# Output transposes moved from TensorE and ScalarE to VectorE, one mask product for two blocks, biases moved to ScalarE, in a two-layer attention and mixture-of-experts kernel

## The chip, the cores and the metric

The kernel runs on one core of a Trainium2 chip. A core has a matrix engine (TensorE, in the profile PE; its weight loads are PEld), three engines for elementwise work (VectorE or DVE, ScalarE or ACT, GpSimd or POOL), a queue engine (SyncE or SP) and 16 DMA engines. Each engine runs its own instruction list in order and waits on semaphores. The metric is the device time of one launch in microseconds (us), lower is better. Three runs of the kernel before took 2808.42, 2810.91 and 2811.84 us, median 2810.91 us.

## The reference: what is computed

The input `x` is 16 sequences of 512 tokens with 128 channels, float32. Two layers follow, and every head has 8 channels:

```python
xn = layernorm(x)                                   # 16 x 512 x 128
# layer 0, attention A: 16 query heads over 4 key/value heads, with biases, softmax over all 512 keys
a  = softmax((xn@wq.T+bq) . (xn@wk.T+bk) / sqrt(8)) . (xn@wv.T+bv) @ wo.T + bo
# layer 0, block M: rmsnorm, keys and values through a latent of 64 channels with a layernorm,
# rotary positions, 16 heads, causal softmax; then 4 experts, each token goes to its best one
latent = layernorm(rms(xn)@Wdkv.T)*ln_g + ln_b
m  = xn + causal_softmax(rope(q) . rope(latent@Wuk.T)) . (latent@Wuv.T) @ Wo.T
m  = m + expert[argmax(rms(m)@gate.T)](rms(m))      # 128 -> 512 -> 128, relu
x  = x + a + m
xn = layernorm(x)
# layer 1, attention B: 16 query heads over one key/value head, with biases; and a gated layer of 384
x  = x + attention_B(xn) + (silu(xn@wg.T) * (xn@wu.T)) @ wd.T
```

## The kernel before: tiling, stages and what sets the order

One sequence of 512 tokens (4 tiles of 128) is a batch; there are 16. A batch passes through three attentions, named M (causal, with the latent), A (grouped) and B (layer 1). The heads of an attention are taken in 4 groups `g` of 4 heads. For each group:

1. `score_max` computes scores of 128 queries against the keys, 16 units `u` a group. TensorE writes them to a PSUM bank with four matmuls side by side, each on 32 columns of the array (`in_columns`). VectorE takes the row maximum (line 972; for M with the causal mask added, line 977).
2. `shift_split` (GpSimd), `shift_turn` (TensorE, ScalarE, SyncE) turn the maxima and put them as rows 72 and 73 of the queries.
3. `score_exp` computes the scores again, transposed and shifted by the maximum, in 16 units a group (10 for M, where two causal blocks share one bank). For M a product of `late_keys` with the identity adds the mask on the diagonal block. ScalarE writes the exponentials to `probs` (line 1217).
4. `probs_v` multiplies them with the values, with a column of ones for the sum, into the one PSUM bank `pv`. It holds two groups, for 32 rows a head: 16 for the even group's values and 16 for the odd group's.
5. After every second group: `out_copy` copies `pv` to `osb` (ScalarE, line 1223), `out_turn` turns it with four 128x128 transposes (TensorE, line 748), and VectorE divides by the sums (lines 985 and 992) into `otok`, tokens on partitions. After both pairs of groups `o_turn` turns `otok` back (TensorE line 623, ScalarE line 1229) into `oT`, and `o_proj` multiplies with the output weights.

So a batch has six `out_copy` and `out_turn`, and three `o_turn`.

The order of the work is a table of times. `stages()` puts each step at a time in units of which a period has 12 (`PERIOD`); one unit is one group of score maxima. `START` places M at 3, A at 7 and B at 23, and `LEAD` adds 1 to every time, so the maxima of M stand at 4 to 8, of A at 8 to 12 and of B at 24 to 28, which is 0 to 4 of the period two periods later. `score_exp` follows `lag` = 1.986 units behind. Every engine runs the steps that it has a part in, in the table's order; `LATE` moves a step's place on one engine alone. One period handles parts of three batches. The walk repeats it 18 times, and the first and the last periods are only partly filled.

PSUM has 8 banks. One is `pv`; the other 7 are handed out round robin in the table's order, with the same banks in every period. `last_user` makes the taker of a bank wait for the step that read it last. A query or key in `full_q` or `full_k` passes through GpSimd's `split` into three bfloat16 parts and by DMA (`pack`) into the operand rows. The table places `m_lat_turn` at 1.55, `o_turn` of A at 2.521, `out_copy` of A at 0.174 and 2.174 (with `LEAD`, modulo 12).

Of the kernel before, what the change touches and what calls it, by code (L numbers as in the profile page):

```python
# [102 lines left out]
for _n, _w in (("a_bv", 32), ("a_bo", 128), ("gate_b", EXPERTS), ("b_bv", HD), ("b_bo", 128)):  # L103
# [36 lines left out]
def stages():  # L140
# [92 lines left out]
def spare_users(name, *args):  # L233
# [8 lines left out]
        "out_turn": [(f"{a}_otok", g + 1)] if name == "out_turn" else [],  # L242
        "o_turn": [(f"{a}_oT", 1)], "o_proj": [({"M": "x2_ready", "A": "gqa_added", "B": "y_ready"}.get(a), 1)],
# [12 lines left out]
def kernel_program(nc, x, w_all, w_lat, v_all, r_all, consts, wx, xq, yq, wi_up, wi_down, rope, out):  # L256
# [7 lines left out]
    with ctx:  # L264
# [64 lines left out]
        otok = sb("otok", [P, TILES, D])  # L329
# [270 lines left out]
        def _(pe):  # L600
# [222 lines left out]
            def ff_down(b):  # L823
                m = misc_bank(b, "res_b", 1)
                pe.wait_ge(sig["ff_hid"], total(b, "ff_hid"))
                for t in range(TILES):
                    for c in range(FCH):
# [12 lines left out]
        def _(v):  # L840
            turn_mx, turn_full, turn_otok, turn_factored = {}, {}, {}, {}
            turn_hid = {}
# [76 lines left out]
            def m_lat_turn(b):  # L919
# [594 lines left out]
```

## Time and profile before

| | |
|---|---|
| median of 3 runs (lowest, highest) | 2810.91 us (2808.42, 2811.84) |
| profiled execution, its own time | 2806.16 us |
| its span, first to last instruction | 2804.4 us |
| PE busy | 2618.0 us, 93% |
| DVE busy | 2303.3 us, 82% |
| ACT busy | 1735.6 us, 62% |
| POOL busy | 813.7 us, 29% |
| mean granted TensorE clock | 0.977 of full |
| DMA | 191.23 MB, mean 68 GB/s |

Busy time is the time in which at least one instruction of the engine is in flight. An instruction's duration contains a tail that overlaps the next one, so that work which is issued back to back takes less than the sum of the durations. The distance from the start of one to the start of the next is then its price. An engine that waits less than such a tail still counts as busy.

### The profile page before, as it was taken

The numbers are of one execution on the slowest core, as the hardware profiler recorded it, in microseconds if no ns is written. First come the engines' busy times: TensorE is split into PE (matmuls) and PEld (weight loads), VectorE is DVE, ScalarE is ACT, GpSimd is POOL, SyncE is SP. The second block draws the span as 40 slices with busy tenths as digits, with TensorE's granted clock in tenths as the row PEclk, the third lists the DMA queues.
The fourth block names the chain that finished last, engine by engine and source line by source line (L and its number), as shares of the span: only waits on it lengthen the run. The fifth ranks groups of instructions, "written<-read, shape, count | busy, mean of one in ns | idle before, by whom it ended". The sixth has DMA issues, their size and how long they took to land. (4 is left out here: it accounts for less than half of the span.)

```text
span 2804.4 us, 120631 instructions
## 1 busy us (share of the span) xinstructions
PE 2618.0 (93%) x50864; PEld 1434.5 (51%) x50864; DVE 2303.3 (82%) x6003; ACT 1735.6 (62%) x3538; POOL 813.7 (29%) x1385
## 2 busy tenths in 40 slices
PE   5969999999999999999999999999999999999958
PEld 2445464645546465464645546464554646456432
DVE  5758889798898979889797987979889897988735
ACT  1725757666576666757666575766757666675825
POOL 4132422223241222423133242222324122242120
PEclk7979999999999999999999999999999999999987
DMA  3041221403112041221304122140312204132120
GB/s 99 7 129 32 79 75 32 125 25 109 54 59 91 26 137 29 90 74 43 106 25 131 36 82 72 32 125 25 110 53 66 83 27 136 28 96 67 39 67 6
DMA packets 168044, 191.23 MB, mean 68 GB/s; under 512 B 24614, under 2 KB 150736, under 8 KB 167504
## 3 DMA queue, kind: packets, MB, share of 16 engines
q1 hardware_dynamic: 163408, 175.12, 20.7%
q0 software_dynamic: 4096, 8.40, 1.1%
q8 instruction: 402, 6.59, 1.0%
q14 instruction: 138, 1.13, 0.1%
HBM read 84.18 MB, written 16.25 MB: 36 GB/s over the span
## 5 line engine op out<-in xcount | busy, mean ns | idle before, releaser
L1217 ACT ACTIVATE probs<-bank 128x512 f32<-128x512 f32 x2688 | 1461.7, 598 | 667.5 <-PE bank L617 661.0
L972 DVE TENSOR_REDUCE mx<-bank 128x1 f32<-128x512 f32 x2048 | 1281.4, 681 | 65.2 <-PE bank L617 52.2
L977 DVE CUSTOM_DVE_ANT_0 bank<-bank,mask 128x128 f32<-128x128 f32 (+3 forms) x1024 | 478.5, 517 | 106.6 <-PE bank L617 100.4
L617 PE MATMUL bank<-kp_B,qp_B 72*32 72x512 bf16 x4096 | 442.9, 392 | 18.8 <-issue 9.4
L617 PE MATMUL bank<-qp_B,kp_B 74*32 74x512 bf16 x4096 | 415.4, 384 | 2.2 <-ACT probs L1217 1.6
L617 PE MATMUL bank<-qp_A,kp_A 74*32 74x512 bf16 x4096 | 408.2, 380 | 6.7 <-DVE mx L972 6.1
L617 PE MATMUL bank<-kp_A,qp_A 72*32 72x512 bf16 x4096 | 384.2, 381 | 14.8 <-DVE mx L972 7.5
L1362 POOL TENSOR_SCALAR nms<-mx 128x16 bf16<-128x16 f32 x192 | 39.8, 207 | 1043.2 <-DVE mx L977 510.2
L617 PE MATMUL bank<-kp_M,qp_M 72*32 72x128 bf16 (+3 forms) x4096 | 314.7, 311 | 28.2 <-DMA kp_M<-parts_k 20.4
L617 PE MATMUL bank<-qp_M,kp_M 74*32 74x512 bf16 (+3 forms) x4096 | 284.8, 302 | 20.3 <-DVE mx L972 15.2
L738 PE MATMUL pv<-probs,vv_B 128*32 128x512 f32 x2048 | 275.6, 596 | 1.2 <-ACT probs L1217 1.0
L738 PE MATMUL pv<-probs,vv_A 128*32 128x512 f32 x2048 | 266.9, 592 | 0.1
L617 PEld LDWEIGHTS bank<-kp_B,qp_B 72*32 72x32 bf16 x4096 | 136.1, 97 | 206.0 <-issue 87.3
L617 PE MATMUL bank<-late_keys,identb 128*32 128x128 bf16 x4096 | 210.5, 220 | 0.8 <-issue 0.6
L617 PEld LDWEIGHTS bank<-qp_B,kp_B 74*32 74x32 bf16 x4096 | 131.1, 97 | 134.4 <-issue 50.5
L617 PEld LDWEIGHTS bank<-qp_A,kp_A 74*32 74x32 bf16 x4096 | 122.2, 97 | 147.2 <-DVE mx L972 42.6
L617 PEld LDWEIGHTS bank<-kp_A,qp_A 72*32 72x32 bf16 x4096 | 109.1, 96 | 158.2 <-DVE mx L972 59.0
L738 PE MATMUL pv<-probs,vv_M 128*32 128x384 f32 (+3 forms) x2048 | 177.2, 435 | 0.3 <-issue 0.2
L617 PEld LDWEIGHTS bank<-qp_M,kp_M 74*32 74x32 bf16 x4096 | 122.9, 96 | 106.6 <-DVE mx L972 44.7
L617 PEld LDWEIGHTS bank<-kp_M,qp_M 72*32 72x32 bf16 x4096 | 122.8, 99 | 104.3 <-issue 54.1
L617 PEld LDWEIGHTS bank<-late_keys,identb 128*32 128x32 bf16 x4096 | 123.2, 98 | 46.3 <-issue 25.2
L977 DVE DVE_READ_ACCUMULATOR2_ANT mx<- 128x1 f32 x1024 | 145.2, 142 | 0.0
(171 smaller groups left out, 3296.6 us busy)
## 6 DMA issues: line engine op xcount, KB each, us to landing
wxs<-wx SPq DMA_DIRECT2D x112, 578.0 KB, 4.3
qp_M<-parts_q SPq DMA_DIRECT2D x144, 128.0 KB
kp_M<-parts_k SPq DMA_DIRECT2D x144, 128.0 KB
qp_A<-parts_q SPq DMA_DIRECT2D x144, 128.0 KB
qp_B<-parts_q SPq DMA_DIRECT2D x144, 128.0 KB
xp<-xq SPq DMA_DIRECT2D x16, 448.0 KB, 7.1
kp_A<-parts_k SPq DMA_DIRECT2D x144, 32.0 KB
xs<-x SPq DMA_DIRECT2D x16, 256.0 KB, 3.0
```

Source lines behind the costliest of these rows:

```text
L617: ins = pe.matmul(dst[at:at + n], lhsT[:, at:at + n], rhs, start=start, stop=stop, tile_position=(0, at))
L738: ins = pe.matmul(pv[0][32 * hh:32 * hh + VW, SEQ - q:SEQ], vv[a][:, c, VHEAD[a](GROUP * g + hh), :], probs[:, SLOT[a, g, u], col:col + q] ...
L972: v.tensor_reduce(mx[:, g % 2, at:at + 1], s1[BANK[a, g, u]][:], AX.X, ALU.max) \
L977: v.tensor_tensor_reduce(bank[:, 0:keys], bank[:, 0:keys], mask[:, SEQ - keys:SEQ], 1.0, LOWEST, ALU.add, ALU.max, mx[:, g % 2, at:at + 1] ...
L1217: act.activation(probs[:, slot, :], s2[BANK2[a, g, u]][:], ACT.Exp).then_inc(sig[f"{a}_exp"], 1)
L1362: chain(b, f"{a}_nms", 2 * g + 1, pool.tensor_scalar(first, top, 1.0, 0.0, ALU.mult, ALU.add))
```

## The change

The diff, cut to its core. The line numbers of the kernel after differ by up to some twenty lines.

```diff
-T = dict(... m_lat=0.995, m_lat_turn=1.55, ...
+T = dict(... m_lat=0.995, m_latn=1.530, m_lat_turn=1.55, ...
...
-        "out_turn": [(f"{a}_otok", g + 1)] if name == "out_turn" else [],
-        "o_turn": [(f"{a}_oT", 1)], "o_proj": ...
+        "o_proj": ...
...
-        otok = sb("otok", [P, TILES, D])
+        otok = sb("otok", [P, SEQ])
...
             def score_exp(b, a, g, u):                      # TensorE
-                for hh, c, col, q in unit_parts(a, u):
+                for part, (hh, c, col, q) in enumerate(unit_parts(a, u)):
...
-                                     True, a != "M")
-                    if a == "M":
-                        ins = in_columns(scores[:, 0:P], identb[:], late_keys[:], False, True)
+                                     part == 0, a != "M")
+                if a == "M":
+                    cols = [col for _, _, col, _ in unit_parts(a, u)]
+                    if len(cols) == 1:
+                        ins = in_columns(s2[BANK2[a, g, u]][:, 0:P], identb[:], late_keys[:], False, True)
+                    else:
+                        blocks = s2[BANK2[a, g, u]][:].rearrange("p (b n) -> p b n", n=P)[:, 0:cols[1] // P + 1:cols[1] // P]
+                        ins = in_columns(blocks, identb[:], late_keys[:].unsqueeze(1).broadcast_to([P, 2, P]), False, True)
...
-            def out_turn(b, a, g):                          # TensorE
-                m = misc_bank(b, f"{a}_otok", g + 1)
-                pe.wait_ge(sig[f"{a}_osb"], total(b, f"{a}_osb", g + 1))
-                for t in range(TILES):
-                    ins = pe.transpose(m[:, P * t:P * t + P], osb[:, g % 2, P * t:P * t + P], ident[:])
-                ins.then_inc(sig[f"{a}_ot_ps"], 1)
-
-            def o_turn(b, a):
-                m = misc_bank(b, f"{a}_oT", 1)
-                pe.wait_ge(sig[f"{a}_otok"], total(b, f"{a}_otok"))
-                turns4(m, otok, f"{a}_oT_ps")
...
+            def m_latn(b):                                  # VectorE, first half of the old m_lat_turn
+                v.wait_ge(sig["lat_rstd"], total(b, "lat_rstd"))
...
+                normed(latn, lat, lmv, lsq[:, 1], "latn_ready")
...
-            def query(b, s, ps, bias):                      # VectorE, and key() alike
-                v.tensor_scalar(full[s[1]][:], misc[SPARE[f"{s}_full", 1]][:], vcol(bias), SCALE,
-                                       ALU.add, ALU.mult).then_inc(sig[f"{s}_full"], 1)
...
+            def out_copy(b, a, g):                          # VectorE
+                v.wait_ge(sig[f"{a}_pv"], total(b, f"{a}_pv", len(CLUSTERS[a]) * (2 * g + 2)))
+                for s_last, value in last_user(b, turn_osb, g % 2, f"{a}_otok", g + 1):
+                    v.wait_ge(s_last, value)
+                v.transpose(osb[:, g % 2, :], pv[0][:]).then_inc(sig[f"{a}_osb"], 1)
+
             def out_turn(b, a, g):
-                v.wait_ge(sig[f"{a}_ot_ps"], total(b, f"{a}_ot_ps", g + 1))
-                m = misc[SPARE[f"{a}_otok", g + 1]][:].rearrange("p (t h c) -> p t h c", t=TILES, c=VHALF)
+                v.wait_ge(sig[f"{a}_osb"], total(b, f"{a}_osb", g + 1))
+                m = osb[:, g % 2, :].rearrange("p (k h c) -> p k h c", h=2, c=VHALF)
...
+            def o_turn(b, a):
+                v.wait_ge(sig[f"{a}_otok"], total(b, f"{a}_otok"))
+                for s_last, value in last_user(b, turn_oT, 0, f"{a}_o_ps", 1):
+                    v.wait_ge(s_last, value)
+                v.transpose(oT[:], otok[:]).then_inc(sig[f"{a}_oT"], 1)
...
-            def out_copy(b, a, g):                          # ScalarE
-                act.activation(osb[:, g % 2, :], pv[0][:], ACT.Copy).then_inc(sig[f"{a}_osb"], 1)
...
-            def o_turn(b, a):
-                act.activation(oT[:], misc[SPARE[f"{a}_oT", 1]][:], ACT.Copy).then_inc(sig[f"{a}_oT"], 1)
...
+            def query(b, s, ps, bias):                      # ScalarE, and key() alike with scale 1
+                act.wait_ge(sig[ps], total(b, ps, 1))
...
+                act.activation(full[s[1]][:], misc[SPARE[f"{s}_full", 1]][:], ACT.Identity, bias=scaled_bias[:, bias:bias + 1],
+                               scale=SCALE).then_inc(sig[f"{s}_full"], 1)
...
-    pair, head, odd, ch_of = np.unravel_index(np.arange(D), (TWOS, GROUP, 2, HD))
+    head, pair, odd, ch_of = np.unravel_index(np.arange(D), (GROUP, TWOS, 2, HD))
```

A VectorE transpose turns every 32x32 block of the tile in its own place. In `pv` a head has 32 partitions, so after it token `32 k + i` of head row block `hh` stands on partition `32 hh + i`, with its 32 channels side by side. The division runs on that layout, and a second block transpose brings `otok` to channels on partitions. The output weights are permuted to match. Below, VectorE at the second `out_copy` and the `o_turn` of A (table times 2.0 to 2.6) in the third period, before and after; `lat`, `latn` and `latT` are the latent, `lg` the gate's logits, `mx` the maxima.

```order
L898 SCALAR_TENSOR_TENSOR rope_s<-bank_5,rot 128x512
L972 TENSOR_REDUCE mx<-bank_6 128x1
L972 TENSOR_REDUCE mx<-bank_1 128x1
L972 TENSOR_REDUCE mx<-bank_3 128x1
L1031 TENSOR_TENSOR lg<-bank_5,row 128x16
L1034 TENSOR_REDUCE lmax<-lg 128x4
L1036 TENSOR_TENSOR eq<-lg,lmax 128x16
L985 RECIPROCAL rc<-bank_6 128x32
L992 TENSOR_TENSOR otok<-bank_6,rc 128x4x64
...
L972 TENSOR_REDUCE mx<-bank_0 128x1
L865 TENSOR_SCALAR latn<-lat,lmv,lsq 128x64 x4
L929 TENSOR_SCALAR latT<-bank_3,vec 64x512
```

The same place on VectorE after the change:

```order
L890 SCALAR_TENSOR_TENSOR rope_s<-bank_4,rot 128x512
L955 TENSOR_REDUCE mx<-bank_5 128x1
L967 STREAM_TRANSPOSE osb<-pv_0 128x512
L955 TENSOR_REDUCE mx<-bank_0 128x1
L955 TENSOR_REDUCE mx<-bank_2 128x1
L1024 TENSOR_TENSOR lg<-bank_4,row 128x16
...
L974 RECIPROCAL rc<-osb 128x32
L980 TENSOR_TENSOR otok<-osb,rc 128x16x16
...
L987 STREAM_TRANSPOSE oT<-otok 128x512
L857 TENSOR_SCALAR latn<-lat,lmv,lsq 128x64 x4
L923 TENSOR_SCALAR latT<-bank_0,vec 64x512
```

Two transposes have come in, one between two maxima and one right ahead of `latn`. Between `latn` and `latT` there is nothing on VectorE, as before. On TensorE, at the end of one period and the start of the next (the first `kp_B` is table time 0), the banks before the change:

```order
L617 MATMUL bank_2<-kp_A,qp_A 32x512 x4
L617 MATMUL bank_3<-qp_A,kp_A 32x512 x4
L738 MATMUL pv_0<-probs,vv_A 32x512 x4
L617 MATMUL bank_4<-kp_A,qp_A 32x512 x4
L617 MATMUL bank_5<-qp_A,kp_A 32x512 x4
L617 MATMUL bank_0<-kp_B,qp_B 32x512 x4
L617 MATMUL bank_1<-qp_A,kp_A 32x512 x4
```

And after the change:

```order
L616 MATMUL bank_0<-kp_A,qp_A 32x512 x4
L616 MATMUL bank_1<-qp_A,kp_A 32x512 x4
L742 MATMUL pv_0<-probs,vv_A 32x512 x4
L616 MATMUL bank_2<-kp_A,qp_A 32x512 x4
L616 MATMUL bank_3<-qp_A,kp_A 32x512 x4
L616 MATMUL bank_0<-kp_B,qp_B 32x512 x4
L616 MATMUL bank_1<-qp_A,kp_A 32x512 x4
```

A period took 426 banks and takes 417. Where the period ends, a bank is now taken again 4 takings later, for four banks; it was 6.

## Rows read from the trace of the kernel before

**Rows 1.** Timeline, VectorE, the latent's copy in two successive periods.

```profile
968.89 0.42 DVE L912 COPY lat<-bank 128x256 f32<-128x256 f32 x1
...
1134.94 0.42 DVE L912 COPY lat<-bank 128x256 f32<-128x256 f32 x1
```

**Rows 2.** Busy time by stretch over one period: stretch, length, each engine's busy us.

```profile
968.90:989.70 20.80, 19.61 (x381) 10.65 (x377) 18.26 (x46) 11.18 (x24) 12.40 (x21) 1.00 0.19 60
989.70:1003.90 14.20, 13.24 (x187) 6.01 (x183) 12.74 (x25) 9.87 (x20) 10.19 (x15) 1.00 0.46 131
1003.90:1029.70 25.80, 25.38 (x543) 14.81 (x538) 19.38 (x79) 19.46 (x41) 4.13 (x8) 1.00 0.47 146
1029.70:1056.30 26.60, 26.48 (x790) 19.91 (x782) 19.57 (x82) 15.12 (x33) 3.76 (x6) 1.00 0.38 114
1056.30:1069.40 13.10, 11.79 (x253) 5.71 (x243) 13.03 (x34) 6.87 (x13) 2.22 (x5) 1.00 0.05 13
1069.40:1087.70 18.30, 17.62 (x359) 10.56 (x363) 15.82 (x28) 8.29 (x16) 10.43 (x14) 1.00 0.15 44
1087.70:1099.80 12.10, 12.10 (x203) 6.07 (x197) 11.17 (x20) 9.21 (x19) 0.00 (x0) 1.00 0.17 44
1099.80:1134.90 35.10, 33.94 (x523) 14.73 (x515) 33.53 (x71) 28.29 (x60) 7.11 (x18) 1.00 0.04 11
```

**Rows 3.** Timeline, TensorE around a transpose of `osb`: start, us, engine, line, operation.

```profile
1057.28 0.40 PE L617 MATMUL bank<-qp_M,kp_M 74*32 74x512 bf16 x4
1057.50 0.24 PE L617 MATMUL bank<-late_keys,identb 128*32 128x128 bf16 x4
1057.56 0.40 PE L617 MATMUL bank<-kp_A,qp_A 72*32 72x512 bf16 x4
1057.89 0.65 PE L748 MATMUL bank<-ident,osb 128*128 128x128 f32 x4
1058.47 0.40 PE L617 MATMUL bank<-kp_A,qp_A 72*32 72x512 bf16 x4
```

**Rows 4.** Timeline, TensorE, a 256-column product.

```profile
1053.47 0.24 PE L617 MATMUL bank<-late_keys,identb 128*32 128x128 bf16 x4
1053.53 0.29 PE L617 MATMUL bank<-qp_M,kp_M 74*32 74x256 bf16 x4
1053.64 0.24 PE L617 MATMUL bank<-late_keys,identb 128*32 128x128 bf16 x4
```

**Rows 5.** Timeline, VectorE, maxima back to back.

```profile
1119.07 2.48 DVE L972 TENSOR_REDUCE mx<-bank 128x1 f32<-128x512 f32 x4 [0.18 <-PE bank L617]
```

**Rows 6.** Groups of instructions: busy us, mean ns of one, idle before them.

```profile
L937 DVE TENSOR_SCALAR full_q<-bank,vec 128x512 f32<-128x512 f32 x32 | 23.9, 746 | 11.8 <-PE bank L617 11.8
L944 DVE TENSOR_SCALAR full_k<-bank,vec 32x512 f32<-32x512 f32 x16 | 11.8, 738 | 4.2 <-PE bank L617 2.9 <-POOL parts_k L1353 1.3
L912 DVE COPY lat<-bank 128x256 f32<-128x256 f32 x16 | 6.8, 425 | 13.8 <-PE bank L617 13.8
L1341 POOL TENSOR_TENSOR full_q<-full_q,rope_s 128x512 f32<-128x512 f32 x16 | 20.6, 1287 | 0.1
```

**Rows 7.** Timeline around the latent's transpose.

```profile
978.51 1.02 DVE L865 TENSOR_SCALAR latn<-lat,lmv,lsq 128x64 f32<-128x64 f32 x4
979.67 0.60 PE L652 MATMUL bank<-ident,latn 128*64 128x128 f32 x4 [1.19 <-DVE latn L865]
980.31 0.80 DVE L929 TENSOR_SCALAR latT<-bank,vec 64x512 f32<-64x512 f32 x1 [0.79 <-PE bank L652]
```

**Rows 8.** Timeline, `out_copy` on ScalarE and what VectorE does there.

```profile
1056.27 3.08 DVE L972 TENSOR_REDUCE mx<-bank 128x1 f32<-128x512 f32 x5
...
1057.03 0.60 ACT L1223 ACTIVATE osb<-pv 128x512 f32<-128x512 f32 x1 [0.29 <-PE pv L738]
```

**Rows 9.** The chain of waits, its last part.

```profile
2796.05 0.61 ACT osb L1223
...
2799.83 1.20 PE bank L617 x32
```

More of the change, by code:

```diff
@@ L241, in spare_users @@
         "shift_turn": [(f"{a}_nmT", g + 1)] if name == "shift_turn" else [],
-        "out_turn": [(f"{a}_otok", g + 1)] if name == "out_turn" else [],
-        "o_turn": [(f"{a}_oT", 1)], "o_proj": [({"M": "x2_ready", "A": "gqa_added", "B": "y_ready"}.get(a), 1)],
+        "o_proj": [({"M": "x2_ready", "A": "gqa_added", "B": "y_ready"}.get(a), 1)],
         "gate": [("logits", 1)],
@@ L833, in _ @@
                          a_q=a_q, a_k=a_k, a_v=a_v, b_q=b_q, b_k=b_k, b_v=b_v, score_max=score_max,
-                         shift_turn=shift_turn, score_exp=score_exp, probs_v=probs_v, out_turn=out_turn,
-                         o_turn=o_turn, o_proj=o_proj, gate=gate, ranks=ranks, xp_turn=xp_turn, up=up, down=down, ff_up=ff_up, ff_down=ff_down)
+                         shift_turn=shift_turn, score_exp=score_exp, probs_v=probs_v, o_proj=o_proj, gate=gate, ranks=ranks, xp_turn=xp_turn, up=up, down=down, ff_up=ff_up, ff_down=ff_down)
             walk(steps, ordered(LATE["PE"]))
@@ L1128, in _ @@
                          m_q=m_q, m_k=m_k, m_lat=m_lat,
-                         m_lat_turn=m_lat_turn,
-                         a_q=lambda b: query(b, "aq", "a_ps", "a_bq"),
-                         a_k=lambda b: key(b, "ak", "a_ps", "a_bk", KCH["A"]),
+                         m_latn=m_latn, m_lat_turn=m_lat_turn,
+                         a_q=lambda b: written_by_act(b, "aq"), a_k=lambda b: written_by_act(b, "ak"),
                          a_v=lambda b: value(b, "A", "a_ps", "a_bv", "av_ready"),
-                         b_q=lambda b: query(b, "bq", "b_ps", "b_bq"),
-                         b_k=lambda b: key(b, "bk", "b_ps", "b_bk", KCH["B"]),
+                         b_q=lambda b: written_by_act(b, "bq"), b_k=lambda b: written_by_act(b, "bk"),
                          b_v=lambda b: value(b, "B", "b_ps", "b_bv", "bv_ready"),
-                         score_max=score_max, out_turn=out_turn, o_proj=o_proj,
+                         score_max=score_max, out_copy=out_copy, out_turn=out_turn, o_turn=o_turn, o_proj=o_proj,
                          x2_norm=x2_norm, gate=gate, route=route, up=up, down=down, moe_added=moe_added,
@@ L1149, in _ @@
             act.wait_ge(setup_pool, 1)
+            for n, bias in enumerate(("a_bq", "b_bq")):
+                ins = act.activation(scaled_bias[:, n:n + 1], vcol(bias), ACT.Copy, scale=SCALE)
+            ins.then_inc(setup_act, 1)
+            act.wait_ge(setup_act, 1)
             def turn(b, what):
@@ L1257, in ff_up, with written_by_dve, key @@
                     .then_inc(sig["tanh_done"], 1)
+            def written_by_dve(b, s):
+                last_user(b, turn_full, s[1], f"{s}_split", 4)
+            def query(b, s, ps, bias):
+                act.wait_ge(sig[ps], total(b, ps, 1))
+                for s_last, value in last_user(b, turn_full, s[1], f"{s}_split", 4):
+                    act.wait_ge(s_last, value)
+                act.activation(full[s[1]][:], misc[SPARE[f"{s}_full", 1]][:], ACT.Identity, bias=scaled_bias[:, bias:bias + 1],
+                               scale=SCALE).then_inc(sig[f"{s}_full"], 1)
+            def key(b, s, ps, bias, n):
+                act.wait_ge(sig[ps], total(b, ps, 2))
+                for s_last, value in last_user(b, turn_full, s[1], f"{s}_split", 4):
+                    act.wait_ge(s_last, value)
+                act.activation(full[s[1]][0:n, :], misc[SPARE[f"{s}_full", 1]][0:n, :], ACT.Identity,
+                               bias=vcol(bias, n)).then_inc(sig[f"{s}_full"], 1)
             walk(dict(turn=turn, x_scaled=x_scaled, x2_scaled=x2_scaled, x1_scaled=x1_scaled,
+                           m_q=lambda b: written_by_dve(b, "mq"), m_k=lambda b: written_by_dve(b, "mk"),
+                           a_q=lambda b: query(b, "aq", "a_ps", 0), a_k=lambda b: key(b, "ak", "a_ps", "a_bk", KCH["A"]),
+                           b_q=lambda b: query(b, "bq", "b_ps", 1), b_k=lambda b: key(b, "bk", "b_ps", "b_bk", KCH["B"]),
                            m_v=m_v, shift_turn=shift_turn,
[L1261 removed]
+                           score_exp=score_exp, xp_turn=xp_turn, up=up,
                            ff_up=ff_up), ordered(LATE["ACT"]))
```

49 lines of the change are left out of this document (17 added, 32 removed).

## The prediction

> **What bounds the kernel now.** I read first how long a period is, then who is busy in each part of it, then what single instructions cost back to back, and last the waits at the places that change.
>
> The latent's copy comes at 968.89 and again at 1134.94 us, so a period lasts 166.05 us [rows 1]. Sixteen batches are worked off, so what a period gains counts about sixteen times. The work of the first and last periods is in that count.
>
> The page has PE busy for 93% of the span and DVE for 82%. An average hides where they meet, so I cut one period into eight stretches, S1 to S8, at the places where a group of score maxima begins on DVE [rows 2]. In table units they are 2-3, 3-4, 4-6, 6-8, 8-9, 9-10, 10-11 and 11-2. The reader is to see the idle time, stretch minus busy time:
>
> - S3 and S4 (maxima of M): PE idle 0.42 and 0.12 us, DVE idle 6.42 and 7.03. TensorE is the bound.
> - S5: DVE idle 0.07 us of 13.1, PE idle 1.31. VectorE is the bound, and the only one.
> - S1, S2, S6, S7, S8: both are short of time. DVE has 2.54, 1.46, 2.48, 0.93 and 1.57 us idle, PE 1.19, 0.96, 0.68, 0 and 1.16.
>
> [...] Seven banks tie the two engines: TensorE can be at most some three maxima ahead, about 2 us. A surplus of one engine in one stretch therefore can't pay for the other's in another. That is the main thing in the forecast: the change takes time from TensorE and gives time to VectorE, and what counts is who was short at each place.
>
> **Prices.** A group of four transposes on TensorE starts at 1057.89 and the next product at 1058.47, which is 0.58 us. The product ahead of it takes 0.33 us instead of the 0.22 of its kind (1057.28 to 1057.50), so the switch costs another 0.11 [rows 3]. A group is 0.69 us of TensorE. There are six of `osb` and three of `otok` in a period: 9 x 0.69 = 6.2 us.
>
> A `late_keys` product of 128 columns takes 0.06 us from its start to the next (1057.50 to 1057.56), a 512-column one 0.22 and a 256-column one 0.11 (1053.53 to 1053.64) [rows 3, 4]. The price follows the columns almost down to 128. Two products become one of 256 columns: 0.12 becomes 0.11. That is 6 of 10 units, 24 a period, 0.2 us. The M stretches give it back in full, but it is small. [...]
>
> A block transpose on VectorE is in no row. VectorE passes 512 columns of PSUM in 0.60 us back to back: four maxima take 2.48 us, of which the last one's duration is 0.68 [rows 5]. Lower end: the 0.43 us of a 256-column copy [rows 6]. Upper end: 1.29 us, which GpSimd takes for 512 columns of a two-input operation [rows 6]. I take 0.60, the row of the same engine and size. Nine of them: +5.4 us. `out_turn` keeps its two operations; that they read SBUF now I cost at nothing, since they are short.
>
> [...]
>
> The biases leave VectorE. `full_q` takes 746 ns and `full_k` 738 [rows 6]; less the overlap of 0.08 us that the maxima show (0.68 against 0.60) that is 0.66 each, and there are four in a period, two in S2 and two in S6: -2.6 us. VectorE is left with +2.8 us a period. ScalarE loses nine copies and gets four operations; it is busy for 62% and idle in every stretch (3.3 us in S2, 10.0 in S6), so I cost it at nothing. If ScalarE came late at `full_q`, the exponentials behind it would wait, but there too it stands right behind TensorE.
>
> **Stretch by stretch.**
>
> - S3: one group of transposes goes (B's first `out_copy`). TensorE is the bound, VectorE's 0.6 us fits into 6.4: -0.6.
> - S4: two groups go, 1.38, and the merged masks: -1.4, less 0.1 for the chain through the experts: -1.3.
> - S5: one block transpose comes in, VectorE has 0.07 us to spare: +0.6. What TensorE saves here is worth nothing.
> - S7: two come in, 1.2 us, against 0.93 idle. TensorE had no idle time and is freed by 1.38, so it falls to second place: +0.3.
> - S8: one comes in, 0.6, against 1.57 idle in three stretches of maxima, which isn't all at the right place: +0.2.
> - S1: two come in. The second (A's `o_turn`) stands right ahead of `latn`. TensorE waits there already: 1.19 us for `latn`, and VectorE then 0.79 us for the transpose [rows 7]. TensorE arrives earlier by up to 1.38, `latn` comes later by up to 1.2, so this wait takes back what the transposes gave. Giving `latn` its own step changes nothing, since nothing stands between it and `latT` on VectorE. +0.2.
> - S2 and S6: VectorE is relieved by 1.3 each, TensorE is not: -0.1 together.
>
> Sum: -0.6 - 1.3 + 0.6 + 0.3 + 0.2 + 0.2 - 0.1 = -0.7 us a period.
>
> Two smaller terms. The banks that held the transposed outputs until VectorE had divided are gone, and with them VectorE's own wait for the transpose: -0.4. At the end of the period banks come round after 4 takings instead of 6, so that TensorE can be only two maxima ahead for a moment: +0.1. Together -1.0 us a period, 16 us in all.
>
> The new wait. `out_copy` on VectorE waits for the last product into `pv`, and behind it are the score maxima, whose banks TensorE needs. On ScalarE the copy began at 1057.03, as soon as `pv` was complete; VectorE began its five maxima at 1056.27, and the copy's place is behind the third of them, 1.8 us later [rows 8]. So `pv` is complete 1.1 us before VectorE gets there, and the wait costs nothing. Its release moves back by that much, while the next product into `pv` comes after some 2 us more of TensorE's work.
>
> At the end of the launch the chain runs from 2796.05 through copy, transposes, division, transposes and copy to `o_proj` at 2799.83, 3.8 us [rows 9]. With two block transposes of some 0.7 us duration and the division it is 2.4 us. That is 1.4 off, and half as much once more in the drain before: 2 us.
>
> So the profiled execution of 2806.2 us would become 2788. The median before is 2810.9, and the same 18 us off it make 2793.
>
> **Rivals.**
>
> A. *VectorE has slack enough and TensorE's relief comes through.* For it: VectorE is idle 22.5 us of 166, and TensorE is 93% busy. Against: the idle time lies in S3 and S4. All 6.2 us would be 99 us; S5 and S1 can't give theirs, so half, 3 us a period: 2811 - 48 = 2763.
>
> B. *A wash.* The wait for `latn` and the end of the period cost 0.5 us each, and S8 the whole 0.6: -1.0 becomes 0. With the end of the launch 2809.
>
> C. *Slower: the block transpose of 4-byte data is slow, and VectorE is the bound.* Place: S5, S7, S8 and S1, where six of the nine stand. Price: at 1.29 us each is 0.69 above mine, 6 x 0.69 = 4.1, less a little where there is idle time, plus 0.2 from S3 and S4. Sum -1.0 + 4.1 = +3.1 a period, 50 us: 2811 + 50 - 2 = 2859. It decides from about 0.77 us start to start on: there six transposes have eaten the gain of 1.0. [...] Against: every VectorE row goes by columns.
>
> D. *Slower by the order alone.* VectorE stands waiting at `out_copy` in S1 and S7, because TensorE, with banks coming round sooner, is not ahead any more; 0.5 us each, plus B: 2825.
>
> **Chances.** Forecast 0.45, A 0.17, B 0.13, C 0.13, D 0.12. What a measurement of this kernel tells from no change is about 0.2%, 5.6 us. Faster by more: forecast and A, and a little of B, 0.62; within 0.2%: most of B and the forecast's edge, 0.13; slower: C, D and the rest, 0.25. The forecast's own range is 2775 to 2804. The range for 8 of 10 takes in most of A and reaches half way to C: 2757 to 2835.
>
> **What would show it.** TensorE's busy time falls by some 90 us and VectorE's rises by some 45. The block transposes' durations lie near 0.7 us, and the maxima behind one start 0.6 us after it. S5 gets longer by 0.6 us and S4 shorter by 1.3. The wait of the latent's transpose for `latn` grows from 1.2 us towards 3. ScalarE's `full_q` shows no long wait. The forecast is wrong if a block transpose lasts over 0.9 us, if VectorE stands idle ahead of it, or if S5 gets shorter.

## The result and the profile after

The changed kernel takes 2877.45 us (median of 6 runs, 2872.43 to 2889.03), the kernel before 2809.66 on the same chip (6 runs). The ratio is 1.0246, 95% interval 1.0229 to 1.0264: slower by 2.5%. The forecast was 2793, with 2835 as the top of its range.

The profiled execution of after is the longest of its runs: 2889.03 us, span 2887.2. First the busy times, part 1 of the page of the kernel after.

```profile
PE 2600.6 (90%) x48752; PEld 1340.7 (46%) x48752; DVE 2358.8 (82%) x6083; ACT 1722.3 (60%) x3460; POOL 811.6 (28%) x1385
```

VectorE is busy 55 us longer, where 45 were forecast. TensorE has 2112 instructions fewer and yet is busy only 17 us less, where 90 were forecast: part of its work must have become slower. Where, the stretches S1 to S8 of one period tell, in the columns of [rows 2].

```profile
990.30:1015.80 25.50, 21.28 (x373) 10.14 (x369) 20.69 (x48) 10.50 (x22) 12.37 (x21) 0.87 0.16 49
1015.80:1030.40 14.60, 13.22 (x184) 5.89 (x180) 11.40 (x23) 11.01 (x22) 10.33 (x15) 1.00 0.44 131
1030.40:1055.50 25.10, 24.84 (x537) 13.93 (x533) 19.73 (x79) 18.96 (x40) 4.02 (x8) 1.00 0.47 149
1055.50:1083.90 28.40, 25.76 (x738) 19.50 (x729) 20.56 (x82) 14.07 (x31) 3.41 (x6) 1.00 0.37 105
1083.90:1097.60 13.70, 11.49 (x222) 4.87 (x215) 13.63 (x34) 6.53 (x12) 2.55 (x5) 1.00 0.05 13
1097.60:1116.00 18.40, 17.73 (x338) 10.47 (x341) 14.80 (x27) 9.61 (x18) 10.37 (x14) 1.00 0.18 49
1116.00:1128.20 12.20, 11.51 (x193) 5.06 (x189) 12.10 (x22) 8.52 (x17) 0.00 (x0) 1.00 0.14 36
1128.20:1163.70 35.50, 34.07 (x521) 13.34 (x515) 34.03 (x73) 28.27 (x59) 7.08 (x18) 1.00 0.04 10
```

S5 is 0.6 us longer, S7 0.1 and S8 0.4, near the +0.6, +0.3 and +0.2 of the prediction. Two rows are far off. S1 is 4.7 us longer and shows a granted clock of 0.87. S4 is longer too (28.4 against 26.6), though TensorE's work in it fell from 26.48 to 25.76.

One period may be an odd one, so I took the same cuts in ten periods of each trace, from the starts of the maxima. Means:

| | period | S1 | S2 | S3 | S4 | S5 | S6 | S7 | S8 |
|---|---|---|---|---|---|---|---|---|---|
| before | 166.55 | 20.8 | 13.3 | 25.8 | 28.0 | 13.1 | 18.4 | 12.1 | 35.1 |
| after | 173.23 | 25.8 | 14.0 | 25.6 | 28.1 | 13.7 | 18.4 | 12.2 | 35.5 |
| forecast difference | -1.0 | +0.2 | -0.1 (with S6) | -0.6 | -1.3 | +0.6 | | +0.3 | +0.2 |
| measured difference | +6.7 | +5.0 | +0.7 | -0.2 | +0.1 | +0.6 | 0 | +0.1 | +0.4 |

[Rows 2] show a period in which S4 was short: 26.6, against 28.0 on the mean. Ten times 6.7 are 67 of the 83 us between the two spans.

Now S1. The timeline of TensorE in the kernel after; the first two rows with brackets are its waits, the second answers to 979.67 in [rows 7].

```profile
999.68 0.40 PE L616 MATMUL bank<-kp_B,qp_B 72*32 72x512 bf16 x4 [1.47 <-DVE mx L955]
999.91 0.39 PE L616 MATMUL bank<-qp_B,kp_B 74*32 74x512 bf16 x4
...
1003.05 1.04 PE L651 MATMUL bank<-ident,latn 128*64 128x128 f32 x4 [2.75 <-DVE latn L857]
1004.02 0.62 PE L616 MATMUL bank<-kp_B,qp_B 72*32 72x512 bf16 x4
1004.42 0.64 PE L616 MATMUL bank<-qp_B,kp_B 74*32 74x512 bf16 x4
1004.85 0.64 PE L616 MATMUL bank<-kp_B,qp_B 72*32 72x512 bf16 x4
```

The wait for `latn` is 2.75 us instead of 1.19. And right behind it a product of 512 columns takes 0.64 instead of 0.39 us, with 0.43 to the next start instead of 0.22: half speed. The windows of the same place, columns as above, have the granted clock behind the busy times:

```profile
1000.00:1003.90 3.90, 1.15 (x12) 0.54 (x4) 2.90 (x8) 0.60 (x1) 1.45 (x8) 0.79 0.30 84
1003.90:1010.80 6.90, 6.90 (x117) 2.77 (x120) 3.80 (x7) 1.79 (x3) 0.00 (x0) 0.62 0.39 127
1010.80:1015.00 4.20, 4.20 (x103) 2.94 (x98) 4.00 (x10) 1.58 (x3) 2.58 (x3) 1.00 0.02 4
```

Behind two waits, 1.47 and 2.75 us, the granted clock is 0.62 on the mean of 6.90 us in which TensorE has no idle time (6.90 of 6.90), and then 1.00 again; from 1003 to 1009 us it is 0.50. Between 210 and 2600 us it falls to 0.50 15 times in the trace, for 109 us in all: at this place in each of the 14 periods that start there, and once in an S3, behind a wait of 2.0 us. In the trace of before there is no fall between these times. If TensorE is the bound all the while, half of the 109 us is lost, about 55; that is an estimate and an upper one.

VectorE at the same place, kernel after and then kernel before, timelines:

```profile
995.55 1.25 DVE L955 TENSOR_REDUCE mx<-bank 128x1 f32<-128x512 f32 x2
996.72 0.16 DVE L1024 TENSOR_TENSOR lg<-bank,row 128x16 f32<-128x16 f32 x1
...
997.12 0.97 DVE L1029 TENSOR_TENSOR eq<-lg,lmax 128x16 f32<-128x16 f32 x1
998.01 0.34 DVE L974 RECIPROCAL rc<-osb 128x32 f32<-128x32 f32 x1
998.38 0.65 DVE L980 TENSOR_TENSOR otok<-osb,rc 128x256 f32<-128x256 f32 x1
998.95 2.47 DVE L955 TENSOR_REDUCE mx<-bank 128x1 f32<-128x512 f32 x4
1001.35 0.70 DVE L987 STREAM_TRANSPOSE oT<-otok 128x512 f32<-128x512 f32 x1
1001.97 0.94 DVE L857 TENSOR_SCALAR latn<-lat,lmv,lsq 128x64 f32<-128x64 f32 x4
```

```profile
975.30 0.17 DVE L1036 TENSOR_TENSOR eq<-lg,lmax 128x16 f32<-128x16 f32 x1
...
975.77 0.43 DVE L992 TENSOR_TENSOR otok<-bank,rc 128x256 f32<-128x256 f32 x1
```

The block transpose has the price of the forecast: 0.70 us, 0.62 from its start to the next. But `eq`, which the change doesn't touch, takes 0.97 instead of 0.17, and `otok` 0.65 instead of 0.43. GpSimd's timeline in the kernel after shows what runs then:

```profile
996.89 1.16 POOL L1354 TENSOR_TENSOR rest<-full_q,parts_q 128x512 f32<-128x512 f32 x1
998.14 0.62 POOL L1355 TENSOR_SCALAR parts_q<-rest 128x512 bf16<-128x512 f32 x1
```

`eq` starts inside `rest` and ends at 998.09, just behind its end at 998.05.

S4 last. Timeline of SyncE's queue in the kernel after (the transfers of the experts' weights), then that of TensorE:

```profile
1056.54 0.35 SPq L540 DMA_DIRECT2D wxs<-wx  x1
...
1061.45 0.35 SPq L540 DMA_DIRECT2D wxs<-wx  x1
```

```profile
1060.95 1.08 PE L616 MATMUL bank<-xpT,wxs 128*32 128x128 f32 x32 [0.98 <-DMA wxs<-wx]
...
1066.22 1.08 PE L616 MATMUL bank<-xpT,wxs 128*32 128x128 f32 x32 [1.13 <-DMA wxs<-wx]
```

TensorE goes on 4.4 and 4.8 us after these issues, and it has waited for the weights for 2.1 us in the stretch.

### The profile page after: what moved, and what is told of

It is laid out like the page before. It is cut to its first block and busy times, and to the rows that moved or that the text cites. A ratio compares the mean times of both kernels' runs of the same rounds, so it can differ in the third digit from the quotient of the medians.

```text
span 2887.2 us, 116265 instructions
## 1 busy us (share of the span) xinstructions
PE 2600.6 (90%) x48752; PEld 1340.7 (46%) x48752; DVE 2358.8 (82%) x6083; ACT 1722.3 (60%) x3460; POOL 811.6 (28%) x1385
## 5 line engine op out<-in xcount | busy, mean ns | idle before, releaser
L616 PE MATMUL bank<-qp_A,kp_A 74*32 74x512 bf16 x4096 | 401.1, 380 | 15.0 <-DVE mx L955 14.3
L616 PE MATMUL bank<-qp_M,kp_M 74*32 74x512 bf16 (+3 forms) x4096 | 265.3, 302 | 26.4 <-DVE mx L955 20.5
L742 PE MATMUL pv<-probs,vv_B 128*32 128x512 f32 x2048 | 287.0, 623 | 1.3 <-ACT probs L1212 1.0
L616 PEld LDWEIGHTS bank<-kp_B,qp_B 72*32 72x32 bf16 x4096 | 125.1, 99 | 274.5 <-DVE mx L955 130.9
L616 PEld LDWEIGHTS bank<-qp_A,kp_A 74*32 74x32 bf16 x4096 | 113.4, 96 | 181.7 <-DVE mx L955 94.1
L616 PEld LDWEIGHTS bank<-qp_B,kp_B 74*32 74x32 bf16 x4096 | 125.3, 99 | 148.9 <-issue 60.8
L616 PE MATMUL bank<-late_keys,identb 128*32 128x128 bf16 (+1 forms) x2560 | 183.1, 253 | 0.7 <-issue 0.7
L742 PE MATMUL pv<-probs,vv_M 128*32 128x512 f32 (+3 forms) x2048 | 179.8, 435 | 3.0 <-issue 2.9
L616 PE MATMUL bank<-xpT,wxs 128*32 128x128 f32 x3584 | 123.2, 276 | 32.6 <-DMA wxs<-wx 28.3
```

The lines of the kernel that those rows point to most:

```text
L616: ins = pe.matmul(dst[at:at + n], lhsT[:, at:at + n], rhs, start=start, stop=stop, tile_position=(0, at))
L742: ins = pe.matmul(pv[0][32 * hh:32 * hh + VW, SEQ - q:SEQ], vv[a][:, c, VHEAD[a](GROUP * g + hh), :], probs[:, SLOT[a, g, u], col:col + q] ...
```

## The experiments

All ratios are to the kernel before, run beside each (its medians were 2809.3 to 2813.5 us). "clock 0.50" is the time at that granted clock between 210 and 2600 us in the profiled execution; period, S1 and S4 are means over ten periods.

| | kernel | median us | ratio, 95% interval | period | S1 | S4 | clock 0.50 |
|---|---|---|---|---|---|---|---|
| | before | 2811 | 1 | 166.6 | 20.8 | 28.0 | 0 |
| | after | 2877.5 | 1.0246 (1.0229 to 1.0264) | 173.2 | 25.8 | 28.1 | 109 |
| x1 | after, latn early | 2844.8 | 1.0104 (1.0059 to 1.0149) | 169.9 | 22.6 | 28.0 | 68 |
| x2 | after, only the transposes | 2881.4 | 1.0255 (1.0224 to 1.0287) | 171.3 | 24.8 | 28.2 | 82 |
| x3 | after, wait filled | 2845.1 | 1.0120 (1.0085 to 1.0154) | 169.7 | 23.1 | 28.0 | 20 |
| x4 | before, latn 3 transposes later | 2869.1 | 1.0200 (1.0167 to 1.0233) | 171.1 | 25.0 | 28.5 | 85 |
| x15 | x4, wait filled | 2834.0 | 1.0074 (1.0055 to 1.0093) | 168.6 | 22.4 | 27.9 | 3 |
| x7 | before, latn 2 transposes later | 2857.0 | 1.0148 (1.0123 to 1.0173) | 170.4 | 24.1 | 28.7 | 61 |
| x8 | before, masks merged | 2804.6 | 0.9976 (0.9959 to 0.9994) | 166.4 | 20.8 | 27.7 | 0 |
| x14 | before, biases on ScalarE | 2813.5 | 0.9999 (0.9989 to 1.0009) | 166.7 | 20.8 | 28.0 | 3 |
| x6 | x1, res0 later | 2860.7 | 1.0159 (1.0124 to 1.0193) | 171.5 | 24.1 | 27.8 | 85 |
| x5 | x1, four weight slots | 2788.8 | 0.9898 (0.9855 to 0.9940) | 166.1 | 21.6 | 25.0 | 44 |
| x9 | before, four slots | 2781.3 | 0.9886 (0.9862 to 0.9909) | 165.0 | 20.8 | 26.5 | 0 |
| x10 | after, four slots | 2829.2 | 1.0053 (1.0027 to 1.0079) | 169.2 | 25.5 | 24.9 | 99 |
| x11 | x5, eq from the bank | 2794.7 | 0.9924 (0.9898 to 0.9951) | 165.9 | 22.1 | 24.9 | 48 |
| x12 | x11, wait filled | 2767.0 | 0.9831 (0.9806 to 0.9856) | 164.5 | 20.8 | 25.3 | 0 |
| x13 | before, four slots, latn early, filled | 2775.4 | 0.9865 (0.9848 to 0.9882) | 164.9 | 20.5 | 26.4 | 0 |
| x16 | x12, biases on VectorE | 2766.7 | 0.9835 (0.9816 to 0.9855) | 164.0 | 20.7 | 25.1 | 0 |

### Which part, and which wait: x1, x2, x4, x7

**x1.** Only latn's place on VectorE:

```diff
-         m_latn=1.530, m_lat_turn=1.55,
+         m_latn=1.400, m_lat_turn=1.55,
```

Theory W (the wait and the clock) has the loss in S1: in TensorE's wait of 2.75 us for `latn`, and in the 3.4 to 10.2 us at a granted clock of 0.50 behind it.

> The changed kernel with one number changed: VectorE's latn step stands at 1.400 instead of 1.530 in the table, so it comes ahead of both of A's last output steps and of two maxima, not behind them. Nothing else moves. [...] With latn early the wait is under 1.5 us, the granted clock stays at 1.00 in the steady periods, S1 falls from 25.5 to about 21 us, a period from 173 to about 168 or less, and the time to some 2810 (16 x 4.2 = 67 us off 2877). Theory L (VectorE's load): the two block transposes more that VectorE has in S1 are the loss, wherever latn stands. Then what stood ahead of latn stands ahead of the next bank's reader, the time stays at 2865 to 2880 and S1 at 24 or more.

S1 fell by 3.2 us and the time by 33: half of the loss, where theory W had all of it. Theory L, VectorE's load wherever `latn` stands, falls with that. The clock still falls in S1 in 10 of the 14 periods, behind two waits that are left close together. TensorE in x1, the timeline:

```profile
1163.68 0.40 PE L616 MATMUL bank<-kp_B,qp_B 72*32 72x512 bf16 x4 [1.49 <-DVE mx L955]
...
1165.26 0.60 PE L651 MATMUL bank<-ident,latn 128*64 128x128 f32 x4 [0.96 <-DVE latn L857]
```

**x2.** Masks and biases as before, the block transposes and the step `m_latn` kept.

> The changed kernel with two of its parts undone: a mask product for each block, and A's and B's bias on VectorE again. What is left are the block transposes and latn as a step of its own. Theory W: VectorE's two transposes in S1 and their wait are unchanged, so the clock still falls once a period and the time is near the changed kernel's, plus the 2.6 us a period that VectorE gets back in S2 and S6, where it is short by part: 2880 to 2900. Theory L (VectorE's load anywhere): with 2.6 us more on VectorE in each period it is 16 x 2.6 = 42 us slower, 2920. A third, M (the other two parts are what hurts, through ScalarE or the masks): it is much faster than 2877, near 2810.

2881, no different from the changed kernel: the transposes, with `latn` as a step of its own, bring the whole loss with them. VectorE's 2.6 us more a period for the biases are not to be seen; theory L had 42 us for them.

**x4, x7.** In the kernel before, `latn` alone made later; x7 has `range(2)` and `spare` for two.

```diff
+        spare = sb("spare", [P, 3, SEQ])
...
+                for n in range(3):
+                    v.transpose(spare[:, n, :], mask[:])
                 normed(latn, lat, lmv, lsq[:, 1], "latn_ready")
```

For x4 theory W has a fall of the granted clock behind the wait once a period, as in the changed kernel. That is put at another 3 us a period on top of the delay of 1.9, an estimate: 2890 us.

> The kernel before with three block transposes of the mask into a spare buffer right ahead of VectorE's latn, nothing else changed: latn is 3 x 0.62 = 1.9 us later, TensorE's wait for it grows from 1.2 to about 3.0 us. [...] Without the clock's part: 2810 + 16 x 1.9 = 2840. If VectorE catches up in the maxima behind: under 2830.

> The kernel before with two block transposes ahead of latn (three in x4): TensorE's wait for latn about 1.2 + 1.25 = 2.4 us. If the clock falls by how long that wait is, there are fewer or shorter falls than in x4 (89 us in the steady periods), the time lies between 2810 and 2869, near 2835. If any longer wait does it, as in x4: 2860.

Of the 5.0 us that S1 lost in the changed kernel, 4.2 are here (x4) without any of its edits. From 0 to 2 transposes S1 grows by 3.3 us, far more than their 1.25; the third adds 0.9. The wait of TensorE for `latn`, over the launch, is in the lists of waits; us in total, times, longest. Before:

```profile
PE bank L652 <- DVE latn L865: 20.1, 16, 3.0
```

after:

```profile
PE bank L651 <- DVE latn L857: 47.3, 16, 5.8
```

x7:

```profile
PE bank L653 <- DVE latn L866: 38.9, 16, 3.5
```

The totals hold two odd waits at the start of the launch; in the 14 periods from 210 us on, the wait is the same in each. One of 1.14 to 1.19 us (before) leaves the granted clock at 1.00. One of 2.36 us (x7) is followed by a fall in 13 of the 14 periods, one of 2.94 us (x4) in all 14. The changed kernel has 2.75 us, and another wait, of 1.48 us, ends 3.4 us earlier; it has falls in all 14 and spends the most time at 0.50 (109 us, against 61 and 85).

### Is it the clock or the wait: x3, x15

VectorE's program is untouched. TensorE multiplies during the wait:

```diff
                 m = misc_bank(b, "latT_ready", 1)
+                blocks = m[:].rearrange("p (b n) -> p b n", n=P)
+                for _ in range(11):
+                    in_columns(blocks, identb[:], late_keys[:].unsqueeze(1).broadcast_to([P, TILES, P]))
                 pe.wait_ge(sig["latn_ready"], total(b, "latn_ready"))
```

> The changed kernel, in which TensorE, having taken the bank for the latent's transposes, multiplies into it 11 times 512 columns (11 x 0.22 = 2.4 us, overwritten afterwards) before it waits for latn. VectorE's work and its order are the same, so latn is as late as before. Theory W, in its part on the clock: TensorE's idle time there is gone, its clock stays at 1.00, and the time falls although work was added: the wait of 1.6 us more a period stays (26 us), the clock's part of 16 x 3 = 48 us goes: about 2830. If the clock does not depend on that idle time, or costs nothing since VectorE is the bound there: no change, 2870 to 2885.

> x4 (the kernel before with three block transposes ahead of latn, 2869) with eleven filling products on TensorE ahead of its wait for latn. VectorE does exactly what it does in x4. Theory W: the delay of latn stays and costs about 1.9 us a period, the falls of the clock go: 2810 + 30 = 2840. If the clock costs nothing, since TensorE waits anyway: 2869.

Added work makes both kernels faster: after by 32 us, x4 by 35 (intervals far apart in both pairs). The timeline of TensorE in x3, and under it the same S1 in x4 and in x15 as windows:

```profile
1162.66 0.39 PE L616 MATMUL bank<-qp_B,kp_B 74*32 74x512 bf16 x4
1163.04 2.56 PE L616 MATMUL bank<-late_keys,identb 128*32 128x512 bf16 x44
1165.71 0.63 PE L654 MATMUL bank<-ident,latn 128*64 128x128 f32 x4
1166.27 0.40 PE L616 MATMUL bank<-kp_B,qp_B 72*32 72x512 bf16 x4
```

```profile
986.80:1010.90 24.10, 21.17 (x381) 10.81 (x377) 20.12 (x50) 11.26 (x24) 12.30 (x21) 0.93 0.16 52
```

```profile
971.40:993.80 22.40, 22.03 (x425) 11.50 (x421) 20.09 (x50) 11.18 (x24) 12.35 (x21) 1.00 0.18 56
```

In x15 the clock stays at 1.00 in S1 in every period, in x3 in 9 of the 14; in the other five it falls for 3.4 us right behind the other wait, the one of 1.48 us, which nothing fills. S1 is 2.7 us shorter in x3 than in the changed kernel, 2.5 in x15 than in x4. What is left of S1 in x15 against before is 1.6 us, near the transposes' own 1.9. So of S1's +5.0 the clock is at least 2.7.

### VectorE and GpSimd: x6, x11

```diff
-T = dict(x_load=-0.9, x_norm=-0.066, res0=1.148,
+T = dict(x_load=-0.9, x_norm=-0.066, res0=1.27,
```

> The changed kernel with latn early (as x1), and GpSimd's operation that adds a_bo to xs (1.27 us) moved from ahead of M's query to behind its parts. VectorE's order is the same. Theory P (VectorE and GpSimd exclude each other): VectorE's eq, two operands in SBUF, takes 0.17 us in the kernel before and 0.98 in the changed one, since it starts while GpSimd's two-operand operation runs, and it ends where that ends. GpSimd's operations now lie some 0.5 us earlier against VectorE's, so eq falls to about 0.4 to 0.6 us, TensorE's wait for the maximum behind it (1.49 us) by as much, and fewer of the falls of the clock are left: S1 22.5 to under 22, 2845 to 2835. If eq's duration has another cause (its operand lmax just written, say) it stays at 0.98.

`eq` did what theory P said: 0.53 us in all but the first and the last batch. The time did not follow: it is 16 us above x1 (the intervals overlap), and S1 is 1.5 us longer. The stall had found the next operation. Timelines of x6, VectorE and then GpSimd:

```profile
992.64 0.54 DVE L1029 TENSOR_TENSOR eq<-lg,lmax 128x16 f32<-128x16 f32 x1
...
995.24 1.95 DVE L857 TENSOR_SCALAR latn<-lat,lmv,lsq 128x64 f32<-128x64 f32 x4
```

```profile
991.97 1.17 POOL L1354 TENSOR_TENSOR rest<-full_q,parts_q 128x512 f32<-128x512 f32 x1
...
995.21 1.27 POOL L1331 TENSOR_TENSOR res<-xs,row 128x512 f32<-128x512 f32 x1
```

The moved operation began 0.03 us ahead of `latn`, whose four instructions then took 1.95 us instead of 0.97, and TensorE waited 1.95 for them.

x11 takes the second SBUF operand away from `eq`, on top of x5 (below):

```diff
-                v.tensor_tensor(lg[:], m,
+                v.tensor_tensor(logits, m,
...
-                v.tensor_reduce(lmax[:], lg[:], AX.X, ALU.max)
+                v.tensor_reduce(lmax[:], logits, AX.X, ALU.max)
...
-                v.tensor_tensor(eq[:], lg[:], spread(lmax[:], EXPERTS), ALU.is_equal)
+                v.tensor_tensor(eq[:], logits, spread(lmax[:], EXPERTS), ALU.is_equal)
```

`logits` is columns 16 to 31 of the same PSUM bank, which is released by `ties` instead of `logits`.

> x5 (latn early, four slots), and VectorE's logits written into the PSUM bank that they come from instead of SBUF, so that eq has one operand in SBUF, not two. Theory P (VectorE's operation with two SBUF operands waits while GpSimd's runs): eq 0.17 us instead of 0.98, TensorE's wait for the maximum behind it 0.7 instead of 1.5, fewer falls of the clock, S1 21.6 to 20.5: 2789 to 2770. If eq waits for something else, it stays at 0.98.

Timelines of x11, VectorE and then GpSimd:

```profile
969.90 0.17 DVE L1030 TENSOR_TENSOR eq<-bank,lmax 128x16 f32<-128x16 f32 x1
...
970.37 0.75 DVE L980 TENSOR_TENSOR otok<-osb,rc 128x256 f32<-128x256 f32 x1
...
972.24 1.31 DVE L857 TENSOR_SCALAR latn<-lat,lmv,lsq 128x64 f32<-128x64 f32 x4
```

```profile
969.68 1.16 POOL L1355 TENSOR_TENSOR rest<-full_q,parts_q 128x512 f32<-128x512 f32 x1
```

`eq` begins inside `rest` here too and still takes 0.17 us, in all 16 batches; in the changed kernel, with both operands in SBUF, it took 0.97. That settles its cause. It bought nothing: `otok` and `latn` now meet GpSimd's operations (0.75 for 0.65, 1.31 for 0.97), and against x5 the intervals overlap. Two ways to take one such stall away, and each time the next operation has it.

### The transfer of the weights: x5, x9, x10

```diff
-WSLOTS, HSLOTS = 3, 3
+WSLOTS, HSLOTS = 4, 3
```

> The changed kernel with latn early (as x1) and four buffers for the experts' weights instead of three. In S4 TensorE got 1.2 us less work, but the stretch stayed at 28.0 to 28.1 us in every kernel so far, with two waits of 1.0 us for the weights' transfer, which is issued when the expert three tiles back is done and takes 4.3 us. Theory T (the transfer's loop sets S4): with a fourth buffer the transfer is issued a tile earlier, the waits go, S4 falls by 1 to 1.5 us, the period by as much, the time to x1's 2845 - 20 = 2825. Theory E (the chain through the experts on TensorE, VectorE and ScalarE itself sets it): the waits turn into waits for hid, S4 stays within 0.3.

> The kernel before with four buffers for the experts' weights instead of three, nothing else. In it TensorE has 0.12 us idle of 26.6 in S4 of a good period, so by TensorE's busy time there is nothing to gain: S4 27.7 to 28.0, 2805 to 2811 (theory B, busy time). Theory T (the weights' loop sets S4's length already there, at 27.97 on the mean of ten periods, and TensorE's work behind it only just fills it): some of it comes back where the stretch lasts 28 and 29 us instead of 26.6: S4 to 26.5, 16 x 1.4 = 22 us, 2788.

> The changed kernel with four buffers for the weights, latn where the change has it. S4 as in x5, 24.95 (3.0 us less a period, 48 us), S1 as in the changed kernel, 25.8, with the falls of the clock: 2877 - 48 = 2829. Against x9 it says what the whole change is worth once the transfer of the weights is out of the way: S4 1.3 us shorter than there (the relief of TensorE that the prediction had), S1 5 us longer.

Theory T holds, by more than it said: S4 falls by 3.0 us in the changed kernel and by 1.5 in the one before. The windows of S4, x5 and then x9:

```profile
1193.90:1218.80 24.90, 24.90 (x737) 20.12 (x729) 20.39 (x84) 14.06 (x31) 3.33 (x5) 1.00 0.33 97
```

```profile
1183.10:1209.40 26.30, 26.30 (x794) 20.05 (x786) 19.54 (x80) 15.16 (x33) 2.38 (x4) 1.00 0.30 90
```

Now TensorE's work does set the stretch, and it is 1.6 us shorter with the change (24.9 against 26.5 in the mean). The relief that the prediction had in S4 exists; with three slots it turned into a wait for the transfer.

### The parts, and all together: x8, x14, x12, x13, x16

**x8**, the merged masks alone, and **x14**, the biases on ScalarE alone, both as the diff of the change has them:

> The kernel before with the mask products of two blocks as one, nothing else. The prediction has 0.2 us a period for it, 3 us: 2807. In S3 and S4, where TensorE is busy throughout. If the products' start to start is not what it costs (an overhead of each): 24 x 0.06 = 1.4 us a period, 2790.

> The kernel before with A's and B's biases on ScalarE, nothing else. The prediction has -0.1 us a period for S2 and S6 together: 2809. In the kernels with it S2 was on the mean 0.3 to 0.7 longer, but their latn was late too. If ScalarE's place in the queue is the cause, S2 is over 13.6 here too and the time 2820.

The masks gave S4 0.2 us a period and the time 0.2%, as forecast. The biases gave nothing, and S2 is 13.3: alone they don't make it grow.

**x12** is x11 with four filling products (`range(4)` in the diff of x3), **x13** the kernel before with four slots, latn early and the same products, **x16** is x12 with the biases back on VectorE:

> x11, and four products of 512 columns on TensorE (0.9 us, overwritten afterwards) ahead of its wait for latn, which is about 1.0 us long there. Theory W: no fall of the clock is left in the steady periods, S1 shorter by another 0.5 to 1 and nothing lost: 10 us under x11. If what is left of the waits is short enough already: the same as x11, within 5 us.

> The kernel before with four slots, latn early and the four filling products, but without the change's own parts: all transposes on TensorE, masks apart, biases on VectorE. Against x12 (2767) it is the worth of the change itself once its wait and the weights' transfer are out of the way. Theory S (the sum of stretches): S4 1.6 us longer than x12 and S3 0.3, S5 0.6, S7 0.1 and S8 0.4 shorter, S1 and S2 alike: 0.8 a period, 2780. If four slots and filling alone do it: 2767.

> x12 with A's and B's biases back on VectorE. If VectorE's 2.6 us matter in S2 and S6: longer there, up to 16 x 1.3 = 20 us, 2785. If the biases were hidden on VectorE, as the prediction has them nearly: 2767 to 2770.

x5, x8, x9, x11 and x13 beat both kernels as well, but x12 is, with x16, the fastest, 2767 us, and four products of nothing are worth 28 us of it against x11 (10 were expected). TensorE in x12, timeline:

```profile
964.36 0.40 PE L616 MATMUL bank<-kp_B,qp_B 72*32 72x512 bf16 x4 [0.79 <-DVE mx L958]
...
964.96 1.05 PE L616 MATMUL bank<-late_keys,identb 128*32 128x512 bf16 x16
966.19 0.63 PE L654 MATMUL bank<-ident,latn 128*64 128x128 f32 x4 [0.19 <-DVE latn L860]
```

S2 is back at 13.3 in it. The change itself, x12 against x13, is worth 8 us at best: their intervals overlap, and x12 has `eq` from the bank besides. By stretches it is S1 +0.3, S3 -0.5, S4 -1.1, S5 +0.6, S6 -0.1, S7 +0.1 and S8 +0.4, in sum -0.4 a period (164.5 against 164.9). x16 is no different from x12.

## Why the prediction was wrong

**Clock.** The forecast has no term for the clock, and this step failed. The 1.00 that [rows 2] show in all eight stretches was read as a property of the kernel; it was a property of its waits. The prediction foresaw that the wait for `latn` "grows from 1.2 us towards 3", and it became 2.75; what that does to the clock, 0.50 behind it in all 14 periods, was not asked. It costs at least 2.7 us a period in S1 (x3), 2.5 in the kernel before under nearly the same wait (x15 against x4).

**S1, +0.2.** It measured +5.0, of which the clock is 2.7. The other 2.3 (x3 against before) are the size of three rows: two block transposes of 0.62 in front of `latn`, 1.25; `eq`, 0.8 longer; `otok`, 0.2 longer. [Rows 7] said already that TensorE waits 1.19 us for `latn`. So VectorE was the bound ahead of it, what is added there comes nearly in full (1.6 of 1.9 us in x15), and TensorE's own relief only lengthens the wait. The prediction named the wait, but set TensorE's relief of up to 1.38 us against `latn`'s delay of up to 1.2, and came to +0.2. VectorE's 2.54 us of idle time in S1 was no reserve either: 0.4 of it lies ahead of `latn`, the rest behind, where VectorE waits for the latent's transpose first.

**`out_turn` from SBUF, at nothing.** Wrong in kind. Both its operands are in SBUF now. Alone `otok` takes the 0.42 us that it took from PSUM (424 ns in the kernel before, 425 in the changed one, medians of 96), but 0.65 beside GpSimd's operations in S1. It costs 1.0 us a period together with `eq`, which the transpose ahead of it pushed into GpSimd's `rest`: it began 0.2 us ahead of `rest` before (975.30 against 975.49 in that trace) and begins 0.2 us behind its start now. In the traces `eq` ends within 0.04 us of GpSimd's operation in the changed kernel, and with one operand in PSUM it takes 0.17 beside the same operation (x11).

**S4, -1.3.** It measured +0.1. The step read TensorE's idle time in one short period (0.12 us) and took TensorE for the only bound. Right behind it stood the weights' transfer, 4.3 us from issue to landing on the page of before. With that out of the way the relief is 1.6 us (x5 and x10 against x9), and the transfer was worth 1.5 us a period to the kernel before as well.

**S2, -0.1.** It measured +0.7. The biases alone are not the cause (x14). A late `latn` alone isn't it either: x2 has it as late and an S2 of 13.3, and x4 and x7 have 13.2. It is 13.3 again in x12, which has the biases on ScalarE and no long wait. No run isolates the cause; it stays open.

**What held.** The transpose's price (0.70 us, 0.62 start to start; forecast 0.60), S5 +0.6, the merged mask, and within 0.2 us S7 and S8. ScalarE and `out_copy` are free or nearly so. (ScalarE's idle time in S2 is 4.3 us by [rows 2], not 3.3; nothing hung on it.) These are groups of the kernel after, ScalarE's query and VectorE's `osb`; behind the bar the idle time ahead of them and what ended it:

```profile
L1249 ACT ACTIVATE full_q<-bank,scaled_bias 128x512 f32<-128x512 f32 x32 | 22.0, 688 | 12.5 <-PE bank L616 12.5
```

```profile
L967 DVE STREAM_TRANSPOSE osb<-pv 128x512 f32<-128x512 f32 x96 | 68.5, 713 | 42.4 <-PE pv L742 42.3
```

ScalarE waits 0.4 us for each `full_q`. VectorE does stand idle at `out_copy`, 1.5 us in the period shown, which the prediction called a sign against it; but it does so in S3, S4 and S8 (0.74, 0.53 and 0.25 us), where TensorE is the bound or nearly, and in x12 TensorE is busy for 24.80 of 24.80 us of S4 with that wait in it. S3 gave 0.2 to 0.5 of its 0.6, and nothing of the 0.4 for the banks was found by itself. With the waits removed the whole change gives 0.4 us a period (x12 against x13), where 1.0 was forecast. Rival C, the slow transpose, was wrong in its mechanism: 0.62 is under its 0.77. Rival D had VectorE idle at `out_copy` in S1 and S7; it is idle there in neither. The 2835 of the range's top left out a price that none of the rivals had.

## What to carry to other kernels

Ask of each wait that a change lengthens what the waiting TensorE does afterwards: here one of 1.2 us left the granted clock at 1.00 (before), and behind one of 2.36 it was 0.50 for 3.4 us or more in 13 of 14 periods (x7); eleven products of no use in the gap took 32 us off the time (x3). An engine's idle time in a stretch is neither slack at the place where work is added nor a measure of what relief is worth; look at which side of the wait it lies, and how soon the next bound (a transfer, a buffer) comes. When work is shifted on VectorE, look what GpSimd does under it: `eq` went from 0.17 to 0.97 us.

## What the runs showed of the hardware

- TensorE's granted clock at 0.50 for 3.4 to 10.2 us around a wait of 2.36 us in 13 of 14 periods (x7) and of 2.94 us in all 14 (x4); never around one of 1.14 to 1.19 (before). A single one of 1.48 us did it in 5 of 14 (x3), two of 1.49 and 0.96 us close together in 10 of 14 (x1); two of 0.79 and 0.19 with products between (x12) never. At 0.50 products of 512 columns start 0.43 us apart, at 1.00 0.22.
- VectorE's operation of 128x16 elements on two SBUF operands: 0.17 us alone (before), 0.54 (x6) and 0.97 (after) beside GpSimd, each time until GpSimd's instruction ended (within 0.04 us); with one operand in PSUM 0.17 beside it too (x11). An operation with a scalar operand, SBUF to SBUF (`latn`), was held up too in x6: the first of its four took 1.28 us where the others took 0.30, and ended within 0.05 us of GpSimd's `res`; the four took 1.95 us instead of 0.97.
- VectorE's 32x32 block transpose of 128x512 fp32: 0.72 us from PSUM, 0.70 from SBUF (after, medians of 96 and 48).
